# The matrix memory's head norm: inverse root of batches 0 to 2 on GpSimd as a power

## The reference, cut to what matters

```python
# L2_xattn_ref, q = layernorm(x), k = v = ctx_2048, NH = 16, dh = 16
C = qk * D
normalizer = jnp.maximum(jnp.abs(C.sum(-1, keepdims=True)), jnp.exp(-max_log_D))
Cn = C / (normalizer + EPS)
h = jnp.einsum('bhst,bhtd->bhsd', Cn, vh)
mu = h.mean(-1, keepdims=True)
var = ((h - mu) ** 2).mean(-1, keepdims=True)
hn = (h - mu) * jax.lax.rsqrt(var + EPS)
hn = hn * ln_scale.reshape(1, nh, 1, dh)
...
x = x + _L2_xattn_ref(_layernorm(x, axis=-1), ctx_2048, ctx_2048, ...)   # block E
x = x + _L2_ffn_ref(_layernorm(x, axis=-1), ...)                         # block F
x = x + _L3_xattn_ref(_layernorm(x, axis=-1), ctx_2048, ...)             # block G
```

## Time and profile before

| what | value |
|---|---|
| median of 3 runs | 1153.6 us (1152.23 to 1154.63) |
| the profiled execution's own time | 1154.67 us |
| its span from first to last instruction | 1152.9 us |
| mean granted TensorE clock | 0.951 of full |
| TensorE busy | 1027.3 us (89%) |
| VectorE busy | 865.1 us (75%) |
| ScalarE busy | 629.6 us (55%) |
| GpSimd busy | 551.0 us (48%) |

### The profile page before, as it was taken

How to read it: one execution, slowest core, us unless ns; L and a number is a source line. 1 busy time by engine, 2 the same in 40 slices (tenths; PEclk the granted TensorE clock), 3 DMA queues, 4 the chain that set the end, 5 groups by cost and what they waited for, 6 DMA issues and landing times.

```text
span 1152.9 us, 18816 instructions
## 1 busy us (share of the span) xinstructions
PE 1027.3 (89%) x6446; PEld 873.4 (76%) x6446; DVE 865.1 (75%) x2151; ACT 629.6 (55%) x1656; POOL 551.0 (48%) x413
## 2 busy tenths in 40 slices
PE   4999999999995796878677989999999999999966
PEld 3548888888885684545445889898889988999955
DVE  4436787776768553569899888888888899888873
ACT  1574444444332252587856556776767666676721
POOL 1416767668552131101235665656555565555550
PEclk9899999999997898897799899999999999999998
DMA  7003011111100010100000201001000101000101
GB/s 255 1 1 103 31 56 30 53 56 47 36 1 25 8 46 1 74 1 1 2 18 6 69 1 37 1 20 38 20 19 2 55 2 37 2 20 1 74 0 37
DMA packets 13679, 37.14 MB, mean 32 GB/s; under 512 B 1344, under 2 KB 5520, under 8 KB 12944
## 3 DMA queue, kind: packets, MB, share of 16 engines
q1 hardware_dynamic: 13584, 35.93, 9.4%
HBM read 34.88 MB, written 1.05 MB: 31 GB/s over the span
## 4 chain that ended last, share of the span: by engine, by line
PE 64%; DVE 19%; ACT 8%; issue 5%; POOL 1%; DMA 1%; SPq 0%; DVEq 0%; ACTq 0%; POOLq 0%
PE bank L680 15%; PE bank L700 7%; PE bank L2050 7%; PE bank L2073 7%; PE bank L1983 7%; PE bank L1958 3%; ACT y L2198 3%; PE bank L1994 3%; PE bank L1041 2%; DVE g_ql L1917 2%; PE bank L1972 1%; PE bank L1056 1%; PE bank L490 1%; PE bank L491 1%; DMA cxT<-in_dram 1%
## 5 line engine op out<-in xcount | busy, mean ns | idle before, releaser
L2198 ACT ACTIVATE y<-bank,g_mx 128x256 f32<-128x256 f32 x256 | 117.5, 486 | 97.8 <-DVE g_mx L2360 97.8
L2479 POOL TENSOR_TENSOR y<-y,g_sm 128x1024 f32<-128x1024 f32 x64 | 120.3, 1900 | 23.5 <-DVE g_sm L2373 23.5
L2455 POOL TENSOR_TENSOR g_c<-arena 128x1024 fp32r<-128x1024 f32 x30 | 64.1, 2135 | 116.4 <-DVE arena L2294 116.4
L2073 PE MATMUL bank<-arena 128*128 128x256 f32 x512 | 116.1, 380 | 0.0
L718 ACT ACTIVATE arena<-arena 128x512 f32<-128x512 f32 x64 | 40.4, 632 | 126.1 <-DVE arena L799 126.0
L2073 PEld LDWEIGHTS bank<-arena 128*128 128x128 f32 x512 | 95.1, 190 | 12.0 <-issue 0.2
L680 PE MATMUL bank<-b_yh,b_wh 128*128 128x512 f32 x256 | 102.3, 400 | 0.2 <-issue 0.2
L680 PE MATMUL bank<-b_yl,b_wh 128*128 128x512 f32 x256 | 101.9, 398 | 0.0
L680 PE MATMUL bank<-b_yh,b_wl 128*128 128x512 f32 x256 | 101.5, 397 | 0.0
L1958 PE MATMUL bank<-cst,y 128*128 128x128 f32 x512 | 73.8, 277 | 17.5 <-DVE x L2282 14.3
L753 POOL TENSOR_TENSOR b_hl<-arena,b_hh 128x512 fp32r<-128x512 f32 x64 | 81.4, 1293 | 9.1 <-ACT b_hh L727 9.1
(11 more groups left out here) (380 smaller groups left out, 3131.5 us busy)
## 6 DMA issues: line engine op xcount, KB each, us to landing
arena<-in_dram SPq DMA_DIRECT2D x37, 512.0 KB, 3.6
arena<-in_dram SPq DMA_DIRECT2D x17, 256.0 KB, 3.9
arena<-in_dram SPq DMA_DIRECT2D x3, 1024.0 KB, 5.0
cx<-in_dram SPq DMA_DIRECT2D x2, 1024.0 KB, 8.4
arena<-in_dram SPq DMA_DIRECT2D x2, 704.0 KB, 7.4
x<-in_dram SPq DMA_DIRECT2D x1, 1024.0 KB, 5.9
cxT<-in_dram SPq DMA_DIRECT2D x1, 1024.0 KB, 11.6
out_dram<-x SPq DMA_DIRECT2D x4, 256.0 KB, 2.2
```

The source lines that it names most:

```text
L2073: m = pe.matmul(o[:, st * 256:st * 256 + 256], g_t[:, c, st * P:st * P + P], keys, start=True, stop=True)
L2198: m = act.activation(g_p[:, c, st, :], o[:, st * 256:st * 256 + 256], ACT.Exp, bias=g_mx[j % 2][:, 2 * c + st:2 * c + st + 1], accum_out=g ...
L2455: pool.tensor_tensor(cat, g_o[j % 2], g_om, ALU.subtract).then_inc(s_gc, 1)
L2479: pool.tensor_tensor(pf, pf, sums, ALU.mult).then_inc(s_gp, 1)
```

## The change

ScalarE no longer makes the inverse root of batches 0, 1 and 2. The call of `E_rstd_act` in rounds 7, 11 and 15 is gone; batch 3 still has it, after the last round. A new function `E_rstd_pool` does two instructions on GpSimd for each of the three batches: a `tensor_scalar` that multiplies by 1/16 and adds 1e-6, and a `tensor_tensor` that raises 32 numbers for each partition to the power -0.5. `E_pool` calls it at three places. Nothing changes on VectorE, TensorE and SP. The semaphores are the same: `s_ev` (`e_head_var`) says that `e_r` holds the variance, `s_er` (`e_head_rstd`) that it holds the inverse root.

```diff
--- before.py
+++ after.py
@@ -1464,8 +1464,15 @@
             act.wait_ge(s_ev, b + 1)
             r_ = e_r[:, :, :]
             act.activation(r_, r_, ACT.Ln, scale=1.0 / DH, bias=e_eps[:, :]).then_inc(s_eln, 1)
-            act.wait_ge(s_eln, b + 1)
+            act.wait_ge(s_eln, 1)
             act.activation(r_, r_, ACT.Exp, scale=-0.5).then_inc(s_er, 1)
+
+        def E_rstd_pool(pool, C, b):
+            pool.wait_ge(s_ev, b + 1)
+            r_ = e_r[:, :, :].rearrange("p q h -> p (q h)")
+            C.do(pool.tensor_scalar(r_, r_, 1.0 / DH, 1e-6, ALU.mult, ALU.add))
+            C.sync()
+            pool.tensor_tensor(r_, r_, mhalf[:, 0:32], ALU.pow).then_inc(s_er, 1)
 
         def E_hT_act(act, c):
             if c >= 2:
@@ -1488,8 +1495,6 @@
                                              bias=e_aT[:, 1, 32 * b + h:32 * b + h + 1]), ("E", "ld", n))
                         if n == 29:
                             E_em_act(act, 1)
-                        if n % 4 == 1 and s_ in (7, 11, 15):
-                            E_rstd_act(act, s_ // 4 - 1)
                 if s_ == 0:
                     E_y_act(act, HIGH)
                 if s_ == 3:
@@ -1607,11 +1612,14 @@
             V.sync()
 
         def E_pool(pool, C):
+            E_rstd_pool(pool, C, 0)
             ln_pool(pool, C, K_F, EPS, batches=(0,))
+            E_rstd_pool(pool, C, 1)
             ln_pool(pool, C, K_G, EPS, twice=True, batches=(0,))
             ln_pool(pool, C, K_F, EPS, batches=(1,))
             centre_w_pool(pool, 0)
             centre_k_pool(pool, 0)
+            E_rstd_pool(pool, C, 2)
             ln_pool(pool, C, K_G, EPS, twice=True, batches=(1,))
             ln_pool(pool, C, K_F, EPS, batches=(2,))
             take(pool, ("E", "hT", 2 * B - 1))
```

## The result

| | kernel before | changed kernel |
|---|---|---|
| median, first comparison | 1152.91 us | 1159.28 us |
| ratio, 95% interval | | 1.0049 (1.0031 to 1.0068) |
| its own time of the profiled execution | 1154.67 us | 1157.03 us |
| its span | 1152.9 us | 1155.2 us |

The changed kernel is slower, by 0.49% in this comparison. It was measured twice more further down: 1.0054 (1.0042 to 1.0066) and 1.0037 (1.0024 to 1.0050). All 17 times of it have a mean of 1158.2 us; 92 times of the kernel before, taken beside it and beside the experiments, have one of 1153.2. That is +5.1 us with an uncertainty of 0.8. Two more times of the kernel before, 2595 and 2598 us, stand far outside the rest and are left out.

What follows compares the result with a forecast made beforehand. VectorE was taken to bound block E's rounds 7 to 15, its delay passing on one for one. Delays of +2.17, +1.21 and +0.91 (+4.3 us) gave 1159.0 for the profiled execution, 1157.9 for the median; range 1155.2 to 1161.5.

Steps and rivals of the forecast that it cites:

- contention: Block E, batches 0 to 2: power slowed by VectorE's work; 1159.2 at 8%, 1164.9 at 1.43; chance 13 in 100.
- clock: TensorE's L1400 in block E runs at its lower clock level after longer idling; 1159.3 us; chance 12 in 100.
- The power: GpSimd's 128x32 power for each batch, extrapolated from three narrower widths: 5.42 us.
- The path: From the end of variance L1590 to the start of head norm L1595: 0.20 + 5.42 + 0.20 = 5.82 us.
- The three terms: Later start of L1595 in batches 0, 1 and 2: +2.17, +1.21 and +0.91 us, together +4.3.
- The waits that go: VectorE's waits for ScalarE ahead of products L1533 vanish: 1.62, 0.74 and 1.05 us, at most 3.41 gained.
- The cover of G's norm: G's batch 0 norm, queued on GpSimd behind batch 1's power, still ends 2.4 us before its reader L271.
- Absorbed: TensorE, freed of waits for ScalarE, gets ahead; VectorE's 3.4 us behind L1400 vanish; 1154.5 us; chance 12 in 100.
- Faster: GpSimd's power has a large fixed part above 16 columns or runs in blocks; 1151.5 us; 4 in 100 including the rule.
- the turning point: Block E's three batches: the sign turns where 3p = 13.17, path p = 4.39, a power of 3.99 us.
- The rule: GpSimd's power would cost about as much as a plain operation, 0.21 us; 1150.2 us; chance 1 in 100.
- the same shift at the end: L2050, block G's products, starts at 613.3 instead of 609.0, and everything behind it shifts alike.

Runs made afterwards that it cites:

- half power: Changed kernel with GpSimd's power on 16 of the 32 columns, so block E's output is wrong: 1151.49 us, ratio 0.9983 to the kernel before.
- the kernel with the call behind the round: Kernel before, with ScalarE's inverse root of batches 0 to 2 called after the round's fourth head instead of the second: 1151.72 us, ratio 0.9989.

## Why the prediction was right

The forecast was 1157.9 us, 4.3 above the median of before, with a range of 1155.2 to 1161.5; measured were 1159.28, 1159.56 and 1157.37. By the times alone this would not show the mechanism: the first two lie on the numbers of two rivals, contention (1159.2) and clock (1159.3). What decides is in the traces, step by step.

- **The power.** Extrapolated from 2, 10 and 16 columns: 5.42 us. Measured: 5.427 to 5.438. The half power, 2.90, lies on the same line. The prediction called the fixed part almost nothing; by its own rows it is some 0.4 us (0.743 - 2 x 0.157 = 0.43, 2.906 - 16 x 0.157 = 0.39). The sum started from the row of 16 columns, which holds it, so this cost nothing.
- **The path.** 5.82 forecast; 5.93, 5.85 and 5.86 measured. The 0.2 us for three hand-overs were 0.16 + 0.09 + 0.03 = 0.28 in batch 0, the `tensor_scalar` 0.22 instead of 0.20.
- **The three terms.** +2.17, +1.21, +0.91 forecast. With the measured paths 5.93 - 3.65 = 2.28, 5.85 - 4.61 = 1.24 and 5.86 - 4.91 = 0.95: 4.47 instead of 4.29.
- **The waits that go.** As said, the 1.62, 0.74 and 1.05 us for ScalarE are gone and the four products run in one piece of 1.94 us. Their end was placed 0.25 us too late, so the idle times came out longer than forecast (4.07, 2.16, 2.17 instead of 3.8, 1.9, 1.9) with the same paths. It didn't enter the sum; it made the limit of the possible gain too small, 3.4 instead of 4.2.
- **The cover of G's norm.** The norm ends at 544.56 + 0.88 = 545.4, its reader L271 starts at 547.65: 2.2 us of cover, forecast 2.4.
- **Contention** (a rival): three powers within 11 ns of each other, though VectorE has work for 1.4 us beside the first and for 3.3 us beside the two others. The products beside them have their 1.94 us. It isn't seen at 32 columns. G's norm behind the power has 0.88 us for two columns where 0.743 is the mean; no run shows why.
- **Clock** (a rival): in part. After 4.80 us of idle time L1400 ran at the lower level, 1.66 instead of 0.94, but VectorE had work for that long. Its waits for L1400 were 1.08 and 2.25 us instead of 0.71 and 2.67, together the same. The third trace of the kernel before shows that the same wait can grow to 4.19 us with no change at all.
- **Absorbed** (a rival): no, for that same sum of 3.3 us; TensorE got ahead of ScalarE's work, not of VectorE's.
- **Faster** (a rival): not at 32 columns. But the half power came out on that side of the turning point, and the turning point of a 3.99 us power lies between it and the whole.
- **The rule** of about 2.6 cycles for an element of a two-input operation (the Trainium skill, "GPSIMD Engine Reference", "3.1 Elementwise — side-by-side cycle accounting"): the product of 32 columns took 0.25 us, the power of the same operands 5.43. The plain operation went from 0.212 us at ten columns to 0.25 at 32, so columns hardly count for it, as by the rule; for the power each counts 0.157 us, and the rule is no guide to it.

The start of block G's products had been forecast for 613.3; it was 612.2, since this execution reached block E's rounds 1.5 us earlier. Counted from the first norm of the ruler it came 142.7 us later, before 138.0: +4.8. The prediction had asked for the same shift at the end, and there the two spans show only 2.3 us: 1.5 went ahead of the block and 0.9 behind L2050. The other two traces of the changed kernel have spans of 1158.0 and 1157.0 us, those of the kernel before 1150.7 and 1153.0; in the mean of three that is +4.5.

## What to carry to other kernels

Before a step is moved to an idle engine, write down for each place how long its result may take before somebody waits: here 3.65, 4.61 and 4.91 us as things stood, and 1.78, 3.61 and 3.61 with the old step gone. A step of 3.1 us on a busy engine was replaced by one of 5.4 on an idle one, 5.9 with the scaling and the hand-overs, and what counts is how that compares with those six: it is longer than each. And look first at what stands behind the step on its old engine: leaving it there and moving the call behind the work that others wait for made the kernel faster by 1.3 us (0.2 to 2.2), in one line.

## What I had not expected of the hardware

- A power on GpSimd costs 0.157 us for each column and some 0.4 beside it, at 2, 10, 16 and 32 columns (0.743, 1.963, 2.906 and 5.43 us); 32 columns cost 0.25 us in all as a product, so the power is 22 times as long. At 32 columns it took the same time in every batch, while powers of two and ten columns sometimes took longer (1.06 and 2.12 us).
- A table load on ScalarE (1.283 us) doesn't wait for the semaphore of the activation behind it. In the kernel with the call behind the round it ran from 516.55 to 517.83 while the variance ended at 517.38, and so hid 0.83 us of its 1.28. In the kernel before, the load of batch 0 had ended at 514.19, ahead of the variance's end at 514.98, and cost the path nothing.
- TensorE's clock is not the same from one execution to the next. In the third trace of the kernel before the sixteen matmuls L1400 at 556.60 took 1.53 us instead of 0.94, VectorE waited 1.5 us longer for them, and the stretch took 122.3 us instead of 120.7, with nothing changed in the kernel. The time ahead of the ruler differed by 3.5 us between traces with the same code there. Two traces are too few to tell an effect of 1 us.
